# Eight pairs of images through a convolution, attention and expert kernel: from a software-pipelined loop over bodies to one written-out list of steps per engine

## What is computed

```python
x = x + _L0_conv_ref(_gn(x), Wg, We, be)          # group norm (32 groups), top 2 of 5 experts, leaky relu
t = _to_tokens(x)                                 # 16 x 256 tokens
t = t + _L1_attn_ref(_ln_t(t), wk, wq, wv, wproj, bproj)   # layer norm, 6 causal heads of 16
t = t + _L1_ffn_ref(_ln_t(t), gate_w, gate_b, w1, b1, w2, b2)  # layer norm, top 2 of 4 experts, 96 -> 384 -> 96, gelu
```

## Time and profile before

| | |
|---|---|
| median of three runs | 435.12 us |
| lowest and highest | 433.81 and 436.12 us |
| span of the profiled execution | 430.4 us |
| PE busy | 348.9 us, 81% |
| DVE busy | 264.2 us, 61% |
| ACT busy | 217.2 us, 50% |
| POOL busy | 101.7 us, 24% |
| DMA, share of 16 engines | 16.6% |

### The profile page before, as it was taken

The page is one execution under the profiler, slowest core; times in us unless marked ns, Lnnn a source line. Parts: engine busy times, 40 slices in busy tenths (PEclk is TensorE's granted clock), DMA queues, the critical chain, the costliest instruction groups (busy, mean ns, idle before and its releaser), DMA issues.

```text
span 430.4 us, 8037 instructions
## 1 busy us (share of the span) xinstructions
PE 348.9 (81%) x2536; PEld 268.5 (62%) x2536; DVE 264.2 (61%) x933; ACT 217.2 (50%) x383; POOL 101.7 (24%) x133
## 2 busy tenths in 40 slices
...
GB/s 177 112 0 0 83 28 2 3 110 0 3 4 108 2 2 29 104 0 4 31 100 0 5 62 68 0 2 0 101 28 2 1 123 7 4 21 0 2 18 20
DMA packets 23930, 14.69 MB, mean 34 GB/s; under 512 B 14145, under 2 KB 23893, under 8 KB 23894
## 3 DMA queue, kind: packets, MB, share of 16 engines
q1 hardware_dynamic: 23894, 14.27, 16.6%
...
## 4 chain that ended last, share of the span: by engine, by line
PE 57%; DVE 11%; SPq 9%; issue 8%; ACT 5%; DMA 5%; POOL 2%; DVEq 0%; POOLq 0%; ACTq 0%
PE PS L715 17%; PE PS L656 8%; SPq L416 7%; PE PS L658 6%; PE PS L657 6%; PE PS L812 4%; DMA k_stack<-qk_parts 3%; ACT prob_a L629 3%; PE PS L772 2%; PE PS L732 2%; PE PS L793 2%; DVE mixed L1045 2%; DVE result L1014 2%; PE PS L759 2%; PE PS L768 1%
## 5 line engine op out<-in xcount | busy, mean ns | idle before, releaser
L715 PEld LDWEIGHTS PS<-w_f,hidden 128*128 128x128 f32 x768 | 93.2, 198 | 0.1
L715 PE MATMUL PS<-w_f,hidden 128*128 128x96 f32 x768 | 93.1, 279 | 0.0
L577 ACT ACTIVATE hidden<-PS 128x512 f32<-128x512 f32 x96 | 56.5, 597 | 54.0 <-PE PS L658 51.7
L1082 DVE TENSOR_REDUCE row_max<-PS 128x2 f32<-128x512 f32 (+2 forms) x80 | 48.4, 635 | 36.3 <-PE PS L763 25.3
L498 POOL TENSOR_TENSOR ln_var<-ln_mv,eps_t 128x4 f32<-128x4 f32 x16 | 3.2, 198 | 179.4 <-DVE ln_mv L979 179.4
L656 PE MATMUL PS<-t_hi,w_hi 128*128 128x512 f32 x96 | 44.5, 463 | 0.6 <-DVE t_lo L1061 0.5
L658 PE MATMUL PS<-t_hi,w_lo 128*128 128x512 f32 x96 | 38.4, 400 | 0.0
L657 PE MATMUL PS<-t_lo,w_hi 128*128 128x512 f32 x96 | 38.2, 398 | 0.0
L987 DVE TENSOR_SCALAR normed<-res,ln_mv,ln_scale 128x96 f32<-128x96 f32 x64 | 22.6, 415 | 25.0 <-POOL ln_scale L501 25.0
L1014 DVE SCALAR_TENSOR_TENSOR result<-PS,weight,result 128x96 f32<-128x96 f32 x96 | 23.7, 309 | 19.0 <-PE PS L715 19.0
L586 ACT ACTIVATE conv_y<-PS 128x486 f32<-128x486 f32 x32 | 18.5, 577 | 27.6 <-PE PS L658 26.5
...
## 6 DMA issues: line engine op xcount, KB each, us to landing
...
```

The lines of the kernel that those rows point to most:

```text
L577: act.activation(hidden[:, m, :], PS[:, HIDDEN_BANKS[m % 2], :], ACT.Gelu).then_inc(h_ready, 1)
L715: mm = pe.matmul(dst, hidden[:, m, t * P:(t + 1) * P], w2_f[:, m, :], start=False, stop=t == TILES - 1 and c == CHUNKS - 1, skip_group_che ...
L1082: dve.tensor_reduce(dst, src, AX_X, ALU.max).then_inc(dve_drained[stage], 1)
```

## The change

The loop and the bodies go. Each engine has one list of `step@n` words for all eight pairs, 438 on PE, 286 on DVE, 324 on ACT, and a plain loop in the program writes its instructions out once. What the steps compute is the same. Steps of different pairs are mixed differently from one part of the list to the next.

```diff
-        def iterations(eng, body, before_second=None):
-            body(0, (FRONT,), 0)
...
-            with eng.Fori(4, PAIRS - 1, 2) as i:
...
+GN_BATCHES = ((0, 2), (2, 8), (8, IMAGES))
+POOLS = {"hidden": (0, 1), "y": (2,), "front": (3, 4), "attn": (5, 6), "tail": (7,)}
+RES1, RES2, T2, WEIGHTS = 3, 3, 2, 3
 ORDER = {
+    PE: """
+        xt@0 xt@1 gavg.0@0 xt@2 xt@3 gavg.1@0 xt@4 xt@5 xt@6 xt@7 gavg.0@1 gavg.1@1 conv.0@0 conv.1@0 conv.2@0
+        conv.3@0 gavg.0@2 gavg.1@2 conv.0@1 conv.1@1 conv.2@1 conv.3@1 conv.0@2 conv.1@2 conv.2@2 conv.3@2 norm1_t@0
+        v@0 qk.0@0 qk.1@0 conv.0@3 conv.1@3 conv.2@3 conv.3@3 norm1_t@1 v@1 qk.0@1 score.0.0@0 score.0.1@0 qk.1@1
+        score.0.2@0 score.0.3@0 conv.0@4 conv.1@4 score.0.4@0 conv.2@4 score.1.0@0 score.1.1@0 conv.3@4 norm1_t@2
+        score.1.2@0 score.1.3@0 score.1.4@0 qk.0@2 qk.1@2 shift@0 score.0.0@1 score.0.1@1 score.0.2@1 score.0.3@1
+        score.0.4@1 score.1.0@1 score.1.1@1 score.1.2@1 prob.0.0@0 prob.0.1@0 prob.0.2@0 score.1.3@1 score.1.4@1
+        prob.0.3@0 prob.0.4@0 prob.1.0@0 prob.1.1@0 prob.1.2@0 prob.1.3@0 prob.1.4@0 shift@1 pv.0@0 pv.1@0 out_t.0@0
+        v@2 out_t.1@0 prob.0.0@1 prob.0.1@1 heads_t@0 prob.0.2@1 prob.0.3@1 proj@0 prob.0.4@1 prob.1.0@1 prob.1.1@1
+        prob.1.2@1 score.0.0@2 pv.0@1 conv.0@5 conv.1@5 conv.2@5 norm2_t@0 out_t.0@1 score.0.1@2 norm1_t@3 ffn1.0@0
+        ffn1.1@0 score.0.2@2 score.0.3@2 qk.0@3 ffn1.2@0 score.0.4@2 ffn1.3@0 ffn1.4@0 score.1.0@2 score.1.1@2
...
+        ffn1.3@6 ffn2.0@6 heads_t@7 ffn1.4@6 ffn1.5@6 proj@7 ffn1.6@6 ffn2.1@6 ffn1.7@6 ffn1.8@6 norm2_t@7 ffn1.9@6
+        ffn1.10@6 ffn2.2@6 ffn1.11@6 ffn1.0@7 gate2@7 ffn1.1@7 ffn1.2@7 ffn2.3@6 ffn1.3@7 ffn1.4@7 ffn1.5@7 ffn1.6@7
+        ffn2.0@7 ffn1.7@7 ffn1.8@7 ffn2.1@7 ffn1.9@7 ffn1.10@7 ffn2.2@7 ffn1.11@7 ffn2.3@7
+        """,
+    VECTOR: """
+        gstat@0 gmean@0 w_conv@0 gvar@0 gstat@1 xn@0 gmean@1 gstat@2 w_qkv@0 gvar@1 gates.0@0 gmean@2 gates.1@0 gvar@2
+        xn@1 mix.1@0 mix.2@0 mix.3@0 xn@2 mix.4@0 stats1@0 xn@3 gates.0@1 norm1@0 gates.1@1 xn@4 gates.0@2 norm1_t@0
+        xn@5 gates.1@2 mix.1@1 mix.2@1 qk.0@0 mix.3@1 mix.4@1 qk.1@0 stats1@1 w_w1@0 norm1@1 mix.1@2 mix.2@2 norm1_t@1
+        xn@6 mix.3@2 mix.4@2 qk.0@1 score.0.0@0 score.0.1@0 qk.1@1 stats1@2 score.0.2@0 score.0.3@0 score.0.4@0
+        norm1@2 score.1.0@0 score.1.1@0 w_gate@0 score.1.2@0 score.1.3@0 norm1_t@2 xn@7 score.1.4@0 shift@0 gates.0@3
+        score.0.0@1 score.0.1@1 qk.0@2 score.0.2@1 score.0.3@1 qk.1@2 score.0.4@1 score.1.0@1 score.1.1@1 gates.1@3
+        score.1.2@1 gates.0@4 mix.1@3 gates.1@4 mix.2@3 score.1.3@1 score.1.4@1 shift@1 mix.3@3 mix.4@3 w_b2@0
+        out_t.0@0 out_t.1@0 mix.1@4 mix.2@4 mix.3@4 proj@0 stats1@3 norm2@0 score.0.0@2 norm1@3 norm2_t@0 score.0.1@2
...
+    SCALAR: """ ... """, GPSIMD: """ ... """, SYNC: """ ... """}
...
-        filled = {g: sem(f"filled_{names[g]}") for g in RING}
+        filled = {kind: sem(f"filled_{kind}") for kind in PER if kind != "gavg"}
...
-        conv_y = sb("conv_y", [P, TILES, CONV_N])
+        conv_ys = [sb(f"conv_y{i}", [P, TILES, CONV_N]) for i in range(2)]
...
+        w1_f = hidden[0:C + 1, 0:CHUNKS, :].rearrange("p a b -> p (a b)").rearrange("p (e h) -> p e h", h=HID)
+        conv_f = hidden[0:C + 1, 3, 0:CONV_N]
```

More of the change, by code:

```diff
@@ L61 @@
 PE, SCALAR, VECTOR, GPSIMD, SYNC = range(5)
 ORDER = {
[L65 to L73, removed]
@@ L80 @@
-    VECTOR: [
-        ("ffn2", 0), ("xn",), ("proj",), ("norm2",), ("ffn2", 1), ("score", 0, 0), ("score", 0, 1),
-        ("norm2_t",), ("gates", 0), ("score", 0, 2), ("score", 0, 3), ("gates", 1), ("score", 0, 4),
-        ("score", 1, 0), ("ffn2", 2), ("score", 1, 1), ("score", 1, 2), ("score", 1, 3), ("score", 1, 4),
-        ("shift",), ("mix", 1), ("mix", 2), ("mix", 3), ("mix", 4), ("stats1",), ("norm1",), ("norm1_t",),
-        ("gate2",), ("qk", 0), ("ffn2", 3), ("out_t", 0), ("out_t", 1), ("qk", 1), ("weights",)],
@@ L86 @@
-    GPSIMD: [
-        ("xn",), ("norm2",), ("norm1",), ("prob", 0, 2), ("prob", 0, 4), ("prob", 1, 2), ("prob", 1, 4),
[L88 to L95, removed]
-UNFUSED = 2
-DRAINS = {"conv": "S", "norm1_t": "SV", "qk": "SV", "v": "S", "score": "V", "shift": "S",
-          "prob": "S", "pv": "S", "out_t": "V", "heads_t": "S", "proj": "V", "norm2_t": "SV", "gate2": "V"}
@@ new lines @@
+POOLS = {"hidden": (0, 1), "y": (2,), "front": (3, 4), "attn": (5, 6), "tail": (7,)}
+POOL_OF = {"xt": "hidden", "gavg": "tail", "conv": "front", "norm1_t": "front", "qk": "front", "v": "front",
+           "score": "attn", "shift": "attn", "prob": "attn", "pv": "attn", "out_t": "attn",
+           "heads_t": "tail", "proj": "tail", "norm2_t": "tail", "gate2": "tail", "ffn1": "hidden", "ffn2": "y"}
+PER = {"xt": 1, "gavg": 1, "conv": TILES, "norm1_t": 1, "qk": 2, "v": 1, "score": 10, "shift": 1, "prob": 10, "pv": 2,
+       "out_t": 2, "heads_t": 1, "proj": 1, "norm2_t": 1, "gate2": 1, "ffn1": BLOCKS, "ffn2": E1}
```

1530 lines of the change are left out of this document (805 added, 725 removed).

## The result

The changed kernel takes 397.0 us at the median of four runs (396.21 to 398.63), against 434.47 us of four runs of the kernel before (432.74 to 436.12): a ratio of 0.9139, with a 95% interval from 0.9105 to 0.9174. The forecast was 395, its range 382 to 412. The profiled execution took 398.63 us and its span is 396.9, so 1.7 us lie outside the instructions.

A forecast was written before the change was run, and what follows sets the result against it. It took DVE to bound the fill and PE the rest: 107 us to the first ffn1, 280 after it, 3.6 for the last DVE step and store, 4.7 from span to median, giving 395 us, range 382 to 412.

The forecast's parts named there:

- The loop: Return from body 5 to body 6: removing the loop saves 7.3 to 8.3 us, bounds 7.3 and 9.5.
- Longer straight code is costed at nothing: Written-out bodies: no added stall; if they stalled as the loop's return does, each time would cost 8 us.
- DVE's work in the fill: Before the first ffn1: 96 us of DVE work against 56 of PE's, so DVE sets the fill.
- The waits in the fill: Before the first ffn1: 11 us of waits (bounds 6 to 18) on top of DVE's sum, putting it at 107.
- The first score at 59: In the fill: pair 0's first score on PE comes at 59 us, against 57.78 before.
- After the fill: From the first ffn1 on: PE bounds; 268.4 us of its work at 95.8% busy take 280, bounds 272.5 to 288.
- Rival 3: After the fill: the order packs better than any stretch now, PE at 98.5%, 384 us; chance 0.13 for 380 to 388.
- Rival 4: After the fill: in-order queues hold each other up, 413 to 464 us; chance 0.12 for 408 to 433, 0.05 for 435 up.
- rival 1: In the fill: DVE slows beside GpSimd, 8 us more, 403; chance 0.2 for 400 to 408, shared with Rival 2.
- Rival 2: In the fill: PE's clock stays at 1.2 GHz, 5 to 8 us more, 402; chance 0.2 shared with rival 1.
- From span to time: Outside the instructions: 4.7 us added to the 390.6 us span to reach the median of the runs, 395.
- The third batch: Group norm in the fill: about 1 us more on DVE, xn@1 and conv@1 earlier; does not end the fill.

The follow-up runs named there:

- e1_unroll: Kernel before with only its loop over bodies written out one after the other; 420.27 us.
- e3_dve_less: Changed kernel without DVE's scaled additions of experts 2 to 4 for pairs 0 to 4, so its result differs; 394.99 us.
- e2: Changed kernel with 69 filler products in PE's idle stretches before the first ffn1, result untouched; 394.04 us.
- e4b: Changed kernel with GpSimd's part of the splits cut to 16 of 512 columns for the early pairs, so its result differs; 392.45 us.
- e7: Changed kernel with qk.0 and qk.1 ahead of v in PE's and ScalarE's lists for pairs 0 and 1; 394.60 us.
- e12: Changed kernel with both reductions at once: fewer DVE scaled additions and GpSimd's splits on 16 of 512 columns; 389.88 us.
- e9: Changed kernel with pair 1's normalised input earlier, q and k before v for pairs 0 and 1, and 87 filler products on PE; 391.05 us.
- e11: Changed kernel without the third product of each ffn1 step for pairs 3 to 5, so its result differs; 390.66 us.
- e5: Changed kernel with group norm in two batches (images 0 and 1, then 2 to 15) instead of three; 401.73 us.

## Why the prediction was right, and where it was not

The forecast of 395 lies 2.0 us below the median, by terms that were wrong in both directions. The sum was 107 + 280 + 3.6 + 4.7; the profiled execution has 118.3 + 275.0 + 3.6 + 1.7 = 398.6.

- **The loop.** Named and placed rightly, sized too small. The prediction gave it 7.3 to 8.3 us, with bounds up to 9.5; e1_unroll gives 12.0 us of span, 14.5 at the median: 10.0 at the return (8.2 of it idle time of PE, 1.8 its work at a lower clock) and some 3 at entry and exit. The forecast did not suffer, because it was summed from work and not as before minus gains. "Longer straight code is costed at nothing" held.
- **DVE's work in the fill.** 96 us forecast, 94.7 measured.
- **The waits in the fill.** This is the term that was mis-sized, and the step that failed. 11 us, bounds 6 to 18, were added to DVE's sum; DVE is idle for 23.6 us ahead of the first `ffn1`, which comes at 118.3, outside the prediction's bounds of 102 to 114. It is not only a size. The prediction took the waits as an addition to a sum that bounds; e3_dve_less takes 13.4 us from the sum and gets 2.3 us of the fill for it. What bounds the fill is a chain of handovers over all engines, in which each link that was shortened gave something: PE at half clock (3.0 us in e2), GpSimd's splits and what they hold up (4.5 in e4b), `v` ahead of `qk` (2.4 in e7), DVE's additions (2.0 in e3, for 13.4 us of work). The gains of DVE and GpSimd add (e12), those of the fillers and the two moves only in part (e9). The prediction had written that it is wrong if DVE is idle in the fill because a chain of handoffs bounds it. For this part that is what happened.
- **The first score at 59.** It came at 67.2. The fronts of pairs 1 and 2, put into pair 0's waits, also stand in front of pair 0's own steps in in-order lists. e7 alone moves the first row maximum from 68.7 to 64.5.
- **After the fill.** PE as the bound is shown by e11 from 239 to 325 us; for the rest it is argued from PE's share. The share was 97.0% where 95.8% was taken, 275.0 us for 280; the 5 us repaid half of the fill's 11. Rival 3's 98.5% was not reached over the whole, but from 280 to 360 us PE is busy for 99.5%, and the loss lies from 160 to 240, at 93.7%. Rival 4 didn't come up: no stretch in the table after is below 93.6%, apart from the last. The prediction's "94 to 98% in every stretch" averaged two different parts.
- **Rivals 1 and 2.** Both act. GpSimd slows single DVE instructions as rival 1 says, 2.01 us for 1.05. It does so at the start too: pair 0's `xn` takes 2.08 us at 11.96, beside GpSimd's memsets, where the kernel before has 0.73. That GpSimd "idles in the fill" was wrong for the start: it is busy for 13.89 of the first 15 us. Rival 2's condition, a low clock in the fill, is what the profile shows (0.75 up to 118.3 us; 1.00 from about 80 was forecast, and from 87 to 103 us it is 0.50), and e2 prices what a part of it costs at 3.0 us. "The new fill keeps PE at work more evenly" was wrong.
- **From span to time.** 4.7 us were added, by setting the median of the runs against the span of an execution that was not among them. The executions whose span and time are both known have 1.7 to 2.7 us outside the span, those of the kernel after and its variants about 1.7. This error of 3 us hid part of the others.
- **The third batch.** About +1 us was written for it, and that it does not end the fill. e5 shows the kernel 4.7 us slower without it; as that run also delays pair 0's conv, the batch's own worth stays open. Not tried: two batches in an order made for them, and the doubled buffers one by one, since the order needs them.

So the range and the side of the forecast were right, and so was PE as the bound where e11 tested it. The explanation of the fill was not. That the forecast came within 2.0 us is luck in part: the fill's 11 us too many were offset by 5 after the fill, by 3 in the step from span to time, and by the 1.6 us between the profiled execution and the median.
